# Normalise-and-transpose in quarters, early weight loads and spread weight-statistics reductions in an attention-plus-FFN layer on eight cores

## The chip, the cores and the metric

One Trainium2 chip, eight cores, one program on all of them, each with its own data: core c works on batch c // 2 and owns the 2048 tokens of one parity of it. Nothing is exchanged between cores. The metric is the device time of the slowest core in microseconds (us).

## What is computed

The reference, cut to what matters (x is 4 x 4096 x 2048, 16 heads of 128, FFN width 5120):

```python
xn = layernorm(x)
q, k, v = xn @ Wq + bq, xn @ Wk + bk, xn @ Wv + bv      # per head, rope on q and k
attn = softmax(q k^T / sqrt(128)) * tril                 # mask after the softmax
a = (attn v) @ Wo + bo
h = square(relu(xn @ tern(w_fc)^T))
f = h @ tern(w_proj)^T
out = x + a + f
# tern(w): am = max(mean|w|, 1e-5); +am where w > 0.7 am, -am where w < -0.7 am, else 0
```

Because the mask comes after the softmax, all 4096 keys enter the denominator of each query, and only the causal ones enter the product with v. Because tern needs mean|w| over a whole matrix, both FFN matrices are read once in full for their sum of magnitudes (the statistics) before they are used.

## The kernel before

The program is written as five lists of closures, one per engine (SyncE, called SP in the profile, GpSimd = POOL, VectorE = DVE, ScalarE = ACT, TensorE = PE), and each engine runs its list in the order in which the Python code appended to it. Semaphores link the lists. So where a statement stands in the Python code sets what it is queued behind. It has stages, with a barrier after the V projection and after the heads, and later ones that the change leaves alone.

**Layernorm (L210 to L298).** 32 blocks of 128 tokens. SP loads x_t (two buffers; load tb waits for the ACT pass of block tb-2, L235), DVE sums (L240), ACT squares with an accumulated sum (L245), small operations give mean and reciprocal deviation, ACT writes xn_t in bf16 (L288), and POOL stores it to a DRAM scratch, xn_scr (L295). xn_t has two buffers, and the ACT pass of block tb waits for the store of block tb-2.

**Transposes (L316 to L327).** When all 32 stores have landed, SP issues 16 transposing DMAs, each of a 4096 x 128 column strip of xn_scr into xnT, which stays in SBUF with channels on partitions. Before them, POOL fetches the bias row bvr and PE and DVE spread it over the partitions (L300 to L315).

**V projection (L329 to L373).** Eight column groups (dch) of 256; POOL loads the weights wv_sl of a group (L339, two buffers, f32 in DRAM and bf16 in SBUF), and for each of 32 token blocks PE runs 16 matmuls (L352), DVE adds the bias into v_ev (L365, two buffers) and POOL stores it to v_scr (L371). The load of group dch stands in POOL's list behind all stores of group dch-1. Then SP loads the rope tables and POOL the q and k weights of head 0 (L385, L391), and a barrier waits for all of it.

**Heads (plan_head, 16 times).** POOL loads the q and k weights (L478, L485). Then come the statistics: 20 pieces of 256 KB per head, loaded by SP into stb (two buffers; load i waits for reduction i-2, emit_stat_load), and reduced by DVE for w_fc (L445, heads 0 to 7) or by ACT for w_proj (L456, heads 8 to 15). All 20 loads and 20 reductions stand at the front of a head's lists; SP's load of v_head (L500) stands behind the loads. After them come the projections. PE makes q in four strips of 512 tokens (L522), in two PSUM banks, so that strip j waits for the ACT eviction (L535) of strip j-2. A pair of strips goes through qe_b, a half swap by two POOL DMAs into qsw_b (L544, L545) and three DVE operations (L553, L554, L562: rope) before the next pair may be evicted into qe_b. The same is done four more times for k (L582, L595, L606, L607, L613, L614, L623). One such pass is called a rope piece here.

Then eight chunks of 256 queries. For each, eight groups of four key blocks: PE makes the scores (L664) in one of three PSUM regions and ACT exponentiates them (L687). Between the groups of chunk c PE does the rest of chunk c-1: the sums of the exponentials (L706), after which DVE masks (L724) and inverts (L759, 1.75 us), then the product with v (L743); DVE scales it (L770) and POOL stores it (L776). The exponentials of groups 0 to 3 of chunk c overwrite what the first half of L743 of chunk c-1 reads, and those of 4 to 7 what its second half reads.

**Later stages.** FFN in (L966), FFN out (L1067), output projection (L1158).

Of the kernel before, what the change touches and what calls it, by code (L numbers as in the profile page):

```python
# [89 lines left out]
def build_nc():  # L90
# [21 lines left out]
    def em(name, fn):  # L112
        streams[name].append(fn)
# [8 lines left out]
    with ExitStack() as S0:  # L122
# [39 lines left out]
        sxnt = dsem("sxnt")  # L162
# [5 lines left out]
        sstat = [dsem("sstat0"), dsem("sstat1")]  # L168
# [42 lines left out]
        with ExitStack() as S1:  # L211
# [13 lines left out]

            LNH = float(H)
            xn_act, xn_store = [], []
            for tb in range(NTB):
# [69 lines left out]
                xn_store.append(sxnc.inc())  # L298

            def f(g):  # L300
                g.dma_start(out=bvr_s[:], in_=d["bvr"]).then_inc(sbv.sem, 16)
            em("gpsimd", f)
            bvl = sbv.inc()
            def f(t, bvl=bvl, const_v=const_v):
                t.wait_ge(sbv.sem, bvl)
                t.wait_ge(sem_v, const_v)
                for j in range(4):
                    ins = t.matmul(psum[:, 2048+j*512:2048+(j+1)*512], ones_rb[0:1, :],
                                   bvr_s[0:1, j*512:(j+1)*512], start=True, stop=True)
                ins.then_inc(sem_t, 1)  # L310
            em("tensor", f); bvt = st.inc()
            def f(v, bvt=bvt):
                v.wait_ge(sem_t, bvt)
                v.tensor_copy(bvb[:], psum[:, 2048:4096]).then_inc(sem_v, 1)
            em("vector", f); bvb_ready = sv.inc()  # L315

            xn_all = (sxn[0].n, sxn[1].n)
            for cb in range(NCB):
                def f(sy, cb=cb, xn_all=xn_all):
                    if cb == 0:  # L320
                        sy.wait_ge(sxn[0].sem, xn_all[0])
                        sy.wait_ge(sxn[1].sem, xn_all[1])
                    sy.dma_start(out=xnT[:, cb*T:(cb+1)*T],  # L323
                                 in_=d["xn_scr"][:, cb*128:(cb+1)*128],
                                 transpose=True).then_inc(sxnt.sem, 16)
                em("sync", f)
                sxnt.inc()  # L327
            xnT_ready = sxnt.n

            wv_load, vproj_mm, vproj_ev, v_store = [], [], [], []  # L330
            for dch in range(8):
                buf = wv_sl[dch % 2]
                sl = d["wv"][:, dch*256:(dch+1)*256].rearrange("(cb p) n -> p cb n", p=128)
                war = (dch - 2 + 1) * NTB - 1 if dch >= 2 else None
                swvc = swv[dch % 2]
                def f(g, sl=sl, buf=buf, war=war, swvc=swvc):
                    if war is not None:
                        g.wait_ge(sem_t, vproj_mm[war])
                    g.dma_start(out=buf[:].rearrange("p (cb n) -> p cb n", n=256),  # L339
                                in_=sl).then_inc(swvc.sem, 16)  # L340
                em("gpsimd", f)
                wv_load.append((swvc.sem, swvc.inc()))
                for tb in range(NTB):
                    bank = (tb % 2) * 512
                    idx = dch * NTB + tb
                    def f(t, dch=dch, tb=tb, bank=bank, idx=idx):
                        t.wait_ge(*wv_load[dch])
                        t.wait_ge(sxnt.sem, xnT_ready)
# [34 lines left out]
            sl = d["wq"][:, 0:128].rearrange("(cb p) n -> p cb n", p=128)  # L383
            def f(g, sl=sl):
                g.dma_start(out=wqk_q[:].rearrange("p (cb n) -> p cb n", n=128),  # L385
                            in_=sl).then_inc(swq.sem, 16)
            em("gpsimd", f)
            wq0_ld = swq.inc()
            sl = d["wk"][:, 0:128].rearrange("(cb p) n -> p cb n", p=128)
            def f(g, sl=sl):  # L390
# [848 lines left out]
```

## Time and profile before

| what | us |
| --- | --- |
| median of the 2 runs shown | 5806.05 (5696.27 and 5915.83) |
| the profiled execution | 5513.23 |
| its span on the slowest core (core 3) | 5511.7 |
| spans of the eight cores | 5440.3 to 5511.7 |

The profile is of core 3. PE is busy for 71% of the span, ACT 28%, DVE 22%, POOL 12%. "Busy" of PE counts overlapped matmuls in a modelled way; what each stage waits for has to be read from its own rows. The engines' idle time is put down to a releaser, the event that came last.

### The profile page before, as it was taken

How to read it: one execution, taken by the hardware profiler on the slowest of the kernel's cores; microseconds unless marked ns; L12 is line 12 of the kernel's file. 1: busy time of each engine (PE TensorE's matmuls, PEld its weight loads, DVE VectorE, ACT ScalarE, POOL GpSimd, SP SyncE). 2: the span in 40 equal slices, each digit the busy share in tenths (PEclk: the TensorE clock that was granted, in tenths of full speed). 3: DMA queues.
4: the chain of work that ended last, by engine and by line, in shares of the span. 5: the costliest groups of instructions: out<-in, count | busy, mean ns of one | idle time of the engine just before them, and what ended most of it. 6: DMA issues, size and time to landing. Idle time of an engine off the chain costs nothing.

```text
span 5511.7 us, 66436 instructions; the slowest of 8 cores (5440.3 to 5511.7 us)
## 1 busy us (share of the span) xinstructions
PE 3927.8 (71%) x23892; PEld 2334.3 (42%) x23892; DVE 1235.9 (22%) x1858; ACT 1570.2 (28%) x2017; POOL 688.2 (12%) x1218
## 2 busy tenths in 40 slices
PE   0058888666676676667666766676788886999788
PEld 0047676434443453345334533453433333444333
DVE  3201112222222222212111211121344440000011
ACT  6400000323432343344434434444333330000000
POOL 0012222000000000000000000000244331000000
PEclk9987789889998898899988988998999998999899
DMA  6751122132123202320232033203355556675664
GB/s 205 201 125 39 41 46 63 43 67 63 26 53 67 61 16 63 67 60 19 62 67 60 14 67 68 58 15 64 122 198 199 186 195 220 227 247 195 187 172 145
DMA packets 364633, 564.40 MB, mean 102 GB/s; under 512 B 226336, under 2 KB 259104, under 8 KB 341024
## 3 DMA queue, kind: packets, MB, share of 16 engines
q1 hardware_dynamic: 228128, 383.90, 23.1%
q0 software_dynamic: 136192, 176.25, 13.0%
q8 instruction: 206, 3.38, 0.3%
q14 instruction: 107, 0.88, 0.1%
HBM read 434.21 MB, written 117.44 MB: 100 GB/s over the span
## 4 chain that ended last, share of the span: by engine, by line
PE 52%; DMA 20%; ACT 9%; DVE 7%; issue 7%; POOL 3%; SPq 2%; ACTq 0%; DVEq 0%; another core or an unknown queue 0%; POOLq 0%
PE psum L1067 9%; PE psum L352 9%; PE psum L706 8%; PE psum L664 7%; PE psum L966 6%; ACT expT L687 5%; DMA stb<-wprT 5%; DMA stb<-wfcT 5%; PE psum L582 4%; PE psum L743 4%; PE psum L1158 4%; DMA qsw_b<-qe_b 2%; DMA x_t<-xp 2%; DMA hT_tc<-hT_scr 2%; SPq L323 2%
## 5 line engine op out<-in xcount | busy, mean ns | idle before, releaser
L687 ACT ACTIVATE expT<-psum 128x1024 bf16<-128x1024 f32 x1024 | 970.1, 1030 | 674.2 <-PE psum L743 620.6
L664 PE MATMUL psum<-qrotT,krotT 128*128 128x256 bf16 x4096 | 611.7, 282 | 377.3 <-ACT expT L687 282.6
L352 PE MATMUL psum<-wv_sl,xnT 128*128 128x256 bf16 x4096 | 516.3, 296 | 169.7 <-DMA xnT<-xn_scr 89.5
L966 PE MATMUL psum<-xnT,qfc 128*128 128x512 bf16 x2560 | 576.4, 388 | 84.7 <-DVE qfc L953 82.3
L664 PEld LDWEIGHTS psum<-qrotT,krotT 128*128 128x128 bf16 x4096 | 365.1, 100 | 564.5 <-issue 515.3
L1067 PE MATMUL psum<-qpr,hT_tc 128*128 128x512 bf16 x2560 | 559.7, 382 | 60.7 <-DMA hT_tc<-hT_scr 60.7
L582 PE MATMUL psum<-xnT,wqk_k 128*128 128x512 bf16 x2048 | 464.4, 387 | 162.4 <-ACT qe_b L535 150.5
L352 PEld LDWEIGHTS psum<-wv_sl,xnT 128*128 128x128 bf16 x4096 | 432.1, 106 | 254.5 <-issue 174.2
L706 PE MATMUL psum<-expT,ones_cb 128*128 128x256 bf16 x4096 | 500.8, 277 | 0.0
L522 PE MATMUL psum<-xnT,wqk_q 128*128 128x512 bf16 x1024 | 276.8, 439 | 294.1 <-DMA wqk_q<-wq 163.8
L706 PEld LDWEIGHTS psum<-expT,ones_cb 128*128 128x128 bf16 x4096 | 405.9, 99 | 52.8
L966 PEld LDWEIGHTS psum<-xnT,qfc 128*128 128x128 bf16 x2560 | 252.8, 100 | 407.9 <-issue 123.7
L1067 PEld LDWEIGHTS psum<-qpr,hT_tc 128*128 128x128 bf16 x2560 | 251.7, 98 | 368.8 <-issue 71.4
L582 PEld LDWEIGHTS psum<-xnT,wqk_k 128*128 128x128 bf16 x2048 | 199.9, 99 | 426.3 <-issue 205.5
L535 ACT ACTIVATE qe_b<-psum,bqc_s 128x512 bf16<-128x512 f32 x64 | 42.0, 684 | 1160.8 <-PE psum L522 915.5
L743 PE MATMUL psum<-expT,v_head 128*128 128x256 bf16 (+1 forms) x2304 | 278.8, 266 | 119.3 <-DVE expT L724 119.2
L522 PEld LDWEIGHTS psum<-xnT,wqk_q 128*128 128x128 bf16 x1024 | 110.8, 110 | 455.8 <-issue 370.7
L743 PEld LDWEIGHTS psum<-expT,v_head 128*128 128x128 bf16 x2304 | 207.6, 97 | 188.5 <-issue 157.5
L776 POOL DMA_DIRECT2D o_scr<-o_sb x128 | 69.9, 546 | 1696.7 <-DVE o_sb L770 1569.4
L1158 PE MATMUL psum<-wo_all,oT_t 128*128 128x512 bf16 x1024 | 232.1, 388 | 52.2 <-DMA wo_all<-wo 52.2
L365 DVE TENSOR_TENSOR v_ev<-psum,bvb 128x256 bf16<-128x256 f32 x256 | 108.7, 425 | 575.8 <-PE psum L352 517.1
L1002 POOL DMA_DIRECT2D hT_scr<-hT_t x320 | 183.1, 580 | 389.1 <-ACT hT_t L993 381.5
(82 smaller groups left out, 2296.5 us busy)
## 6 DMA issues: line engine op xcount, KB each, us to landing
hT_tc<-hT_scr SPq DMA_DIRECT2D x32, 2560.0 KB, 12.6
stb<-wfcT SPq DMA_DIRECT2D x160, 256.0 KB, 3.0
stb<-wprT SPq DMA_DIRECT2D x160, 256.0 KB, 3.0
wpr_b<-wprT SPq DMA_DIRECT2D x40, 1024.0 KB, 5.0
wfc_b<-wfc SPq DMA_DIRECT2D x40, 1024.0 KB, 7.2
x_t<-xp SPq DMA_DIRECT2D x32, 1024.0 KB, 8.2
qsw_b<-qe_b POOLq DMA_DIRECT2D x192, 128.0 KB, 2.4
qpr_scr<-qprs POOLq DMA_DIRECT2D x160, 128.0 KB, 2.2
```

Of the source, the lines that this page charges most:

```text
L323: sy.dma_start(out=xnT[:, cb*T:(cb+1)*T], in_=d["xn_scr"][:, cb*128:(cb+1)*128], transpose=True).then_inc(sxnt.sem, 16)
L352: ins = t.matmul(psum[:, bank:bank+256], xnT[:, cb*T + tb*128: cb*T + (tb+1)*128], wv_sl[dch % 2][:, cb*256:(cb+1)*256], start=(cb == 0), ...
L522: ins = t.matmul(psum[:, bank:bank+512], wqk_q[:, cb*128:(cb+1)*128], xnT[:, cb*T + j*512: cb*T + (j+1)*512], start=(cb == 0), stop=(cb == ...
L582: ins = t.matmul(psum[:, bank:bank+512], wqk_k[:, cb*128:(cb+1)*128], xnT[:, cb*T + tcol: cb*T + tcol + 512], start=(cb == 0), stop=(cb == ...
L664: ins = t.matmul(psum[:, reg+pos*256: reg+pos*256+256], krotT[:, kb*128:(kb+1)*128], qrotT[:, c*W:(c+1)*W], start=(pos % 2 == 0), stop=(po ...
L687: s.activation(expT[:, g0*W:(g0+4)*W], psum[:, reg:reg+1024], AF.Exp, scale=SCALE).then_inc(sem_s, 1)
L706: ins = t.matmul(psum[:, DF0:DF0+W], ones_cb[:], expT[:, kb*W:(kb+1)*W], start=(kb == 0), stop=(kb == 31))
L743: ins = t.matmul(psum[:, OT0+cs:OT0+256], v_head[:, kb*128:(kb+1)*128], expT[:, kb*W+cs:(kb+1)*W], start=(half == 0 and i == 0), stop=(hal ...
L966: ins = t.matmul(psum[:, reg + tc*512: reg + (tc+1)*512], qfc[fb % 2][:, cb*128:(cb+1)*128], xnT[:, cb*T + tc*512: cb*T + (tc+1)*512], sta ...
L1002: g.dma_start(out=d["hT_scr"][tcx][:, fb], in_=hT_t[fb % 2][:, tcx*256:(tcx+1)*256]).then_inc(shc.sem, 16)
L1067: ins = t.matmul(psum[:, reg:reg+512], lhs, qpr[q % 2][:, fb*512:(fb+1)*512], start=(fb == 0), stop=(fb == NFB-1))
L1158: t.matmul(psum[:, reg + cc*512: reg + (cc+1)*512], lhs, wo_all[:, ob*H + cc*512: ob*H + (cc+1)*512], start=(ob == 0), stop=False)
```

## The change

Line numbers of the changed kernel stand in the diff's own rows only; the prose keeps those of the kernel before. What it does:

- bvr, its matmuls and its copy, the first two loads of wv_sl and the q and k weights of head 0 go to the front of the lists, ahead of the layernorm.
- The transposes are cut into four quarters of 1024 tokens. After each eighth block of the layernorm loop, SP waits for the stores of all blocks so far and issues 16 transposes of 1024 x 128. Each quarter has a semaphore of its own, and a V-projection block waits for its own quarter alone.
- stb has three buffers. The 20 loads still stand at the front of a head on SP, while the reductions are taken from a list (RQ) between the groups of the chunk loop by reds_until: after group g of chunk c, (8c + g) * 20 // 64 of them are done.
- v_head is loaded by POOL, behind the q and k weights and ahead of the swaps.

```diff
+            emit_wv_load(0)
+            emit_wv_load(1)
+            sl = d["wq"][:, 0:128].rearrange("(cb p) n -> p cb n", p=128)
...
             for tb in range(NTB):
...
+                if (tb + 1) % 8 == 0:
+                    qt = tb // 8
+                    snap = (sxn[0].n, sxn[1].n)
+                    sxq = sxnt[qt]
+                    def f(sy, qt=qt, snap=snap, sxq=sxq):
+                        sy.wait_ge(sxn[0].sem, snap[0])
+                        sy.wait_ge(sxn[1].sem, snap[1])
+                        for cb in range(NCB):
+                            sy.dma_start(out=xnT[:, cb*T + qt*1024: cb*T + (qt+1)*1024],
+                                         in_=d["xn_scr"][qt*1024:(qt+1)*1024,
+                                                         cb*128:(cb+1)*128],
+                                         transpose=True).then_inc(sxq.sem, 16)
+                    em("sync", f)
...
             for dch in range(8):
+                if dch >= 2:
+                    emit_wv_load(dch)
                 for tb in range(NTB):
+                    qrd = xnq_ready[tb // 8]
-                        t.wait_ge(sxnt.sem, xnT_ready)
+                        t.wait_ge(*qrd)
...
-            stb = [E2(nc.sbuf_tensor(f"stb{i}", [128, 512], F32)) for i in range(2)]
+            stb = [E2(nc.sbuf_tensor(f"stb{i}", [128, 512], F32)) for i in range(3)]
...
                 for k in range(20*h, 20*h+20):
                     emit_stat_load(k)
-                    emit_stat_red(k)
+                RQ = list(range(20*h, 20*h+20))
+                def reds_until(done_groups, RQ=RQ):
+                    tgt = (done_groups * 20) // 64
+                    while (20 - len(RQ)) < tgt:
+                        emit_stat_red(RQ.pop(0))
...
-                em("sync", f)
+                    g.dma_start(out=v_head[:].rearrange("p (kb n) -> p kb n", n=128),
+                                in_=src).then_inc(svh.sem, 16)
+                em("gpsimd", f)
...
                     emit_group(c, 2)
+                    reds_until(c*8 + 3)
                     emit_group(c, 3)
...
                     emit_group(c, 4)
+                    reds_until(c*8 + 5)
                     emit_group(c, 5)
...
                     emit_group(c, 6)
+                    reds_until(c*8 + 7)
                     emit_group(c, 7)
+                    reds_until(c*8 + 8)
                 emit_p2(NCH-1)
+                while RQ:
+                    emit_stat_red(RQ.pop(0))
```

SP's list at the layernorm; L235 and L281 are the loads of x_t, L323 and L353 the transposes. Before:

```order
L235 DMA x_t<-xp 128x2048 x32
L323 DMA_TRANSPOSE xnT<-xn_scr 128x4096 x16
L378 DMA cos_s<-cos 128x4096
L379 DMA sin_s<-sin2s 128x4096
L435 DMA stb<-wfcT 128x512 x20
```

Now:

```order
L281 DMA x_t<-xp 128x2048 x8
L353 DMA_TRANSPOSE xnT<-xn_scr 128x1024 x16
L281 DMA x_t<-xp 128x2048 x8
L353 DMA_TRANSPOSE xnT<-xn_scr 128x1024 x16
L281 DMA x_t<-xp 128x2048 x8
L353 DMA_TRANSPOSE xnT<-xn_scr 128x1024 x16
L281 DMA x_t<-xp 128x2048 x8
L353 DMA_TRANSPOSE xnT<-xn_scr 128x1024 x16
```

The ninth load of x_t now stands behind the first 16 transposes, and so at each of three places.

ACT's list in a head of the second half of the heads, from the evictions of the head before it on; L456 and L469 are the reductions. Before:

```order
L595 ACTIVATE qe_b<-psum,bkc_s 128x512 x8
L687 ACTIVATE expT<-psum 128x1024 x64
L456 ACTIVATE dmp,prr<-stb 128x512 x20
L535 ACTIVATE qe_b<-psum,bqc_s 128x512 x4
L595 ACTIVATE qe_b<-psum,bkc_s 128x512 x8
```

Now, its first two chunks and a little more:

```order
L553 ACTIVATE qe_b<-psum,bqc_s 128x512 x4
L613 ACTIVATE qe_b<-psum,bkc_s 128x512 x8
L705 ACTIVATE expT<-psum 128x1024 x5
L469 ACTIVATE dmp,prr<-stb 128x512
L705 ACTIVATE expT<-psum 128x1024 x2
L469 ACTIVATE dmp,prr<-stb 128x512
L705 ACTIVATE expT<-psum 128x1024 x4
L469 ACTIVATE dmp,prr<-stb 128x512
L705 ACTIVATE expT<-psum 128x1024 x2
L469 ACTIVATE dmp,prr<-stb 128x512
L705 ACTIVATE expT<-psum 128x1024 x3
L469 ACTIVATE dmp,prr<-stb 128x512
```

The 20 reductions left the front and stand singly among the exponentials; DVE's are spread in the same manner in the first eight heads.

POOL's list between the V projection and the first swaps. Before:

```order
L371 DMA v_scr<-v_ev 128x256 x32
L385 DMA wqk_q<-wq 128x16x128
L391 DMA wqk_k<-wk 128x16x128
L544 DMA qsw_b<-qe_b 64x1024
```

Now:

```order
L396 DMA v_scr<-v_ev 128x256 x32
L517 DMA v_head<-v_scr 128x32x128
L562 DMA qsw_b<-qe_b 64x1024
L563 DMA qsw_b<-qe_b 64x1024
```

The two weight loads have gone ahead of the layernorm, and the load of v_head stands directly ahead of the first swap.

## Rows read from the trace of the kernel before

**Rows 1.** Windows by stage: length, busy us of PE, PEld, DVE, ACT, POOL, PEclk, DMA, GB/s.

```profile
0.00:243.00 243.00, 0.00 (x0) 0.00 (x0) 88.91 (x135) 150.88 (x161) 19.04 (x38) 1.00 0.67 208
243.00:336.00 93.00, 1.86 (x4) 0.42 (x4) 2.29 (x1) 0.00 (x0) 0.00 (x0) 1.00 1.01 192
336.00:945.00 609.00, 516.30 (x4096) 432.11 (x4096) 108.67 (x256) 0.00 (x0) 148.53 (x265) 0.83 0.20 46
945.00:2427.00 1482.00, 1003.76 (x6738) 640.13 (x6739) 380.67 (x684) 549.51 (x612) 101.00 (x173) 0.90 0.23 51
2427.00:3920.00 1493.00, 1023.28 (x6848) 651.96 (x6846) 279.43 (x542) 660.91 (x924) 104.40 (x177) 0.91 0.24 52
```

**Rows 2.** Waits of PE over the span: total us, times, longest.

```profile
PE psum L664 <- ACT expT L687: 282.6, 427, 2.0
...
PE psum L522 <- DMA wqk_q<-wq: 163.8, 15, 11.9
...
PE psum L522 <- ACT qe_b L535: 117.4, 8, 16.7
PE psum L352 <- DMA xnT<-xn_scr: 89.5, 1, 89.5
...
PE psum L352 <- DMA wv_sl<-wv: 78.3, 7, 11.4
...
PE psum L522 <- DMA wqk_k<-wk: 12.8, 1, 12.8
```

**Rows 3.** Timeline, end of the layernorm: start, length, engine, operation.

```profile
233.65 1.91 ACT L245 ACTIVATE dump<-x_t 128x2048 bf16<-128x2048 f32 x1 [1.35 <-DMA x_t<-xp]
...
237.74 2.10 ACT L288 ACTIVATE xn_t<-x_t,negmr,rstd 128x2048 bf16<-128x2048 f32 x1 [0.41 <-DVE negmr L277]
...
243.49 91.03 SPq L323 DMA_TRANSPOSE xnT<-xn_scr  x16
```

**Rows 4.** DMA issues: queue, count, KB each, median us to landing.

```profile
x_t<-xp SPq DMA_DIRECT2D x32, 1024.0 KB, 8.2
qsw_b<-qe_b POOLq DMA_DIRECT2D x192, 128.0 KB, 2.4
...
v_scr<-v_ev POOLq DMA_DIRECT2D x256, 64.0 KB, 1.8
v_head<-v_scr SPq DMA_DIRECT2D x16, 1024.0 KB, 7.3
...
wv_sl<-wv POOLq DMA_DIRECT2D x8, 1024.0 KB, 9.1
wqk_q<-wq POOLq DMA_DIRECT2D x16, 512.0 KB, 8.7
```

**Rows 5.** Groups over the span: count, busy us, mean ns, idle before and its releasers.

```profile
L456 ACT ACTIVATE dmp<-stb 128x512 bf16<-128x512 f32 x160 | 101.0, 631 | 220.5 <-DMA stb<-wprT 218.8
...
L535 ACT ACTIVATE qe_b<-psum,bqc_s 128x512 bf16<-128x512 f32 x64 | 42.0, 684 | 1160.8 <-PE psum L522 915.5 <-DVE qrotT L562 245.3
...
L456 ACT ACTIVATION_READ_ACCUMULATOR dmp<-stb 128x1 f32 x160 | 30.1, 188 | 0.0
```

**Rows 6.** Waits in heads 0 to 7 (945 to 2427 us).

```profile
ACT qe_b L535 <- DVE qrotT L562: 190.8, 8, 30.8
```

**Rows 7.** Timeline of DVE, front of head 3.

```profile
1542.54 0.69 DVE L445 TENSOR_REDUCE fcr<-stb 128x1 f32<-128x512 f32 x1 [0.17 <-DMA stb<-wfcT]
1543.14 0.68 DVE L553 TENSOR_TENSOR rt<-qe_b,cos_s 128x1024 bf16<-128x1024 bf16 x1
```

**Rows 8.** Timeline of PE, front of head 10.

```profile
3186.50 9.93 PE L522 MATMUL psum<-xnT,wqk_q 128*128 128x512 bf16 x32 [11.86 <-DMA wqk_q<-wq]
3208.85 9.00 PE L522 MATMUL psum<-xnT,wqk_q 128*128 128x512 bf16 x32 [12.42 <-ACT qe_b L535]
```

**Rows 9.** Chain of waits in the chunk loop of head 10.

```profile
3308.38 1.95 ACT expT L687 x2
```

More of the change, by code:

```diff
@@ L161, in build_nc @@
         sbv = dsem("sbv")
-        sxnt = dsem("sxnt")
+        sxnt = [dsem(f"sxnt{i}") for i in range(4)]
         swv = [dsem("swv0"), dsem("swv1")]
@@ L224, in build_nc, with f @@
             v_ev = [E1(nc.sbuf_tensor(f"v_ev{i}", [128, 256], BF16)) for i in range(2)]
+            def f(g):
+                g.dma_start(out=bvr_s[:], in_=d["bvr"]).then_inc(sbv.sem, 16)
+            em("gpsimd", f)
+            bvl = sbv.inc()
+            def f(t, bvl=bvl, const_v=const_v):
+                t.wait_ge(sbv.sem, bvl)
+                t.wait_ge(sem_v, const_v)
+                for j in range(4):
+                    ins = t.matmul(psum[:, 2048+j*512:2048+(j+1)*512], ones_rb[0:1, :],
+                                   bvr_s[0:1, j*512:(j+1)*512], start=True, stop=True)
+                ins.then_inc(sem_t, 1)
@@ new lines, in build_nc, with f, emit_wv_load @@
+            em("tensor", f); bvt = st.inc()
+            def f(v, bvt=bvt):
+                v.wait_ge(sem_t, bvt)
+                v.tensor_copy(bvb[:], psum[:, 2048:4096]).then_inc(sem_v, 1)
+            em("vector", f); bvb_ready = sv.inc()
+            wv_load, vproj_mm, vproj_ev, v_store = [], [], [], []
+            def emit_wv_load(dch):
+                buf = wv_sl[dch % 2]
+                sl = d["wv"][:, dch*256:(dch+1)*256].rearrange("(cb p) n -> p cb n", p=128)
+                war = vproj_mm[(dch - 1) * NTB - 1] if dch >= 2 else None
+                swvc = swv[dch % 2]
+                def f(g, sl=sl, buf=buf, war=war, swvc=swvc):
+                    if war is not None:
+                        g.wait_ge(sem_t, war)
+                    g.dma_start(out=buf[:].rearrange("p (cb n) -> p cb n", n=256),
+                                in_=sl).then_inc(swvc.sem, 16)
+                em("gpsimd", f)
+                wv_load.append((swvc.sem, swvc.inc()))
@@ new lines, in build_nc, with f @@
+            emit_wv_load(0)
+            emit_wv_load(1)
+            sl = d["wq"][:, 0:128].rearrange("(cb p) n -> p cb n", p=128)
+            def f(g, sl=sl):
+                g.dma_start(out=wqk_q[:].rearrange("p (cb n) -> p cb n", n=128),
+                            in_=sl).then_inc(swq.sem, 16)
+            em("gpsimd", f)
+            wq0_ld = swq.inc()
+            sl = d["wk"][:, 0:128].rearrange("(cb p) n -> p cb n", p=128)
+            def f(g, sl=sl):
+                g.dma_start(out=wqk_k[:].rearrange("p (cb n) -> p cb n", n=128),
+                            in_=sl).then_inc(swk.sem, 16)
@@ L298, in build_nc @@
                 xn_store.append(sxnc.inc())
[L300 to L325, printed above, removed]
-                em("sync", f)
-                sxnt.inc()
@@ L328, in build_nc @@
-            xnT_ready = sxnt.n
-            wv_load, vproj_mm, vproj_ev, v_store = [], [], [], []
-            for dch in range(8):
[L332 to L342, printed above, removed]
+                if (tb + 1) % 8 == 0:
[11 more added lines that the diff above has]
+                    em("sync", f)
+                    for _ in range(NCB):
+                        sxq.inc()
+                    xnq_ready.append((sxq.sem, sxq.n))
@@ L515, in f @@
                         if h == 0 and j == 0:
-                            t.wait_ge(sxnt.sem, xnT_ready)
+                            for _sw, _sv in xnT_ready:
+                                t.wait_ge(_sw, _sv)
                         if j == 0 and qkb_war is not None:
```

45 lines of the change are left out of this document (17 added, 28 removed).

## The prediction

> **What bounds the kernel now.** I read the windows by stage first [rows 1]. In the first 336 us PE does nothing: 243 us are layernorm with the DMA engines busy for 0.67 of the time, then come 93 us in which nothing runs but the transposes, at a DMA share of 1.01 and 192 GB/s. The V projection takes 609 us with 516 us of PE work. The heads take 1482 and 1493 us, some 186 us each, with only 1004 and 1023 us of PE work: the heads hold about 950 us of idle PE. The stages behind them are not touched. Next I read who PE waits for [rows 2]. Of the heads' waits, 282.6 us go to the exponentials, in short pieces (427 times), 163.8 us to the load of the q weights (about 11 us a head), and 117.4 us in eight long pieces to the eviction of q. In the V projection there are seven waits for wv_sl, 11 us each. Last I read a head's front on the engine that is late there. In heads 0 to 7 the first rope operation starts right behind the last reduction of DVE [rows 7], though its q strips were ready long before. In heads 8 to 15 PE makes two q strips and then stands for 12.4 us, because the eviction is queued behind ACT's reductions [rows 8].
>
> So two things the change touches are on the path: the transposes, and a head's front. The question is what it puts on the path in their place.
>
> **The layernorm and its transposes.** Now PE starts V at 336 us, after 89.5 us of waiting for xnT [rows 1, 2]. In the changed order SP's loads stand behind the transposes three times. One stop is priced so. After the last ACT pass ended (237.74 + 2.10 = 239.84 us) SP went on at 243.49: 3.65 us until the store had landed [rows 3]. A quarter of the transposes is a quarter of SP's 91.03 us [rows 3], 22.8 us, if their price goes by bytes; it is the nearest row, and the full DMA share of that window speaks for bytes. Then x_t needs 8.2 us to land [rows 4]. Together 34.6 us, against the 1.35 us that ACT stood idle before the last block [rows 3]: 33 us each, 99 us for three. From below, a price by bytes can hardly fall, as the share is 1 already; from above, it is 5.7 us an instruction whatever its size (91.03 / 16), which makes a quarter 91 us. I take 22.8.
>
> At the start, POOL's queue now holds two wv_sl loads and the q and k loads ahead of the first store of xn. By [rows 4] they are 9.1 us each and 8.7 us for a pair of half that size that shares the queue: some 27 us alone, and more beside the x_t loads. Block 2 can't be written before store 0 has landed. Bounds are 0 (all of it in the 33% of DMA time that is free) and 27 us; I take 15.
>
> Layernorm on DVE thus ends 114 us later, at about 351 us. Does PE start earlier on the first quarters? Only by two blocks: V's evictions stand on DVE behind the whole layernorm loop, and there are two banks. Two blocks are 2 x 516.3 / 256 = 4 us [rows 1]. So V starts in effect at 347 us, 10 us later than now; the last quarter's 22.8 us are hidden behind the 24 blocks (48 us) on the other three. While they run, stores of v_ev slow down; I add 5 us. Then two gains: the second wv_sl load is there already (one of seven waits, -11 us [rows 2]), and the 12.8 us wait for head 0's weights shrinks to the landing of the last store, eviction and issue included about 4.5 us (v_scr lands in 1.8 us [rows 4]), -8 us. **This part: +15 - 11 - 8 = -4 us**, between -30 and +220.
>
> *A page's figure beside this.* The trace moved the transposes at 192 GB/s [rows 1]. The Trainium skill, page "DMA: Bandwidth & Descriptors", section "Latency and other measured facts", gives an effective 261 GB/s for a transposing DMA with a non-contiguous middle dimension. By that figure, an estimate, a quarter would take 17 us and the sum fall by 17 us more; the trace doesn't bear it out here, and the sum goes by the trace.
>
> **The front of heads 0 to 7.** The eviction of the third q strip waits for the first rope piece: 190.8 us in these eight heads [rows 6], against 245.3 over all sixteen [rows 5], so 54.5 us in the other eight, where DVE was free. With reductions gone from DVE's front the first eight should wait like the others: **-136 us** (190.8 - 54.5), 17 us a head. The rope pieces behind it cycle through qe_b, the swap and DVE, and keep their rhythm. Spread out, a reduction takes 0.69 us [rows 7] in a DVE that is busy for 381 of 1482 us [rows 1]; each stands where DVE's next mask or scaling still waits for PE. I cost them at 0; if that cover fails, 160 of them are 110 us.
>
> **The front of heads 8 to 15.** PE waited 117.4 us for the q eviction [rows 2], all of it behind ACT's reductions. Next late is the first rope piece, which moves with the eviction. **-117 us.** But ACT now has the reductions inside the loop, 631 + 188 = 0.82 us each [rows 5]. In a chunk the chain runs through the exponentials of groups 4 to 6 (1.95 us for two of them in one link [rows 9]), while those of groups 0 to 3 and 7 lie beside PE work, with ACT idle behind them until the product with v frees their buffer. Of the four places, the one behind group 4 is on that chain; the rule (8c + g) * 20 // 64 fills it in each of the eight chunks, and in chunk 0 one more stands where ACT alone is the pace. Nine a head: 9 x 0.82 x 8 = **+59 us**. Bounds are 0 and all twenty, 131 us; nine is the count that the chain gives.
>
> **v_head behind POOL.** It takes 7.3 us to land [rows 4], and is first needed behind all projections of the head. But the first swap stands behind it. The q weights land, PE makes two strips (9.93 us [rows 8]), ACT evicts: the swap comes about 11 us after the q weights. In that time the k weights (11.5 us, issued right behind: about 4 us behind the q weights [rows 4]) and v_head (7.3) have to pass, 11 to 12 us. I take 2 us of delay a head, **+32 us**, between 0 and 7.3 us (+117). In return the weights no longer share the DMA engines with the statistics: I let the q load (8.7 us [rows 4]) fall to the 7.3 us that v_head's megabyte takes, 1.4 x 15 = **-21 us**, between 0 and twice that.
>
> **Sum.** -4 - 136 - 117 + 59 + 32 - 21 = -187 us on the profiled execution's 5513.2 us: 5326 us, 0.966 of it. The median of the two runs shown lies 5% above the profiled execution, and I take the ratio over to it: 5806 x 0.966 = **5609 us**.
>
> **Rivals.**
>
> *A: the transposes are priced by the instruction (slower).* At 5.7 us each a stop is 68 us longer, three are +205 us, and the last quarter (91 us) outlasts the 48 us of V work by some 43 us: the sum becomes -187 + 205 + 43 = +61 us, 5574 us, or 5870 us at the median. For it speaks that the 16 instructions took about equal times; against it, the DMA share of 1.01, which an issue limit would not give. It decides from about 4.5 us an instruction on.
>
> *B: the loop and the swap eat it.* All twenty ACT reductions count (+72 us more) and v_head stands fully before the first swap (+85 more): -30 us, 5483 us, or 5774 us at the median; half of this already leaves less than 2%. For it speaks that PE waits 427 times for exponentials [rows 2]. Against it, ACT is busy for only 661 of 1493 us in these heads [rows 1]. The Trainium skill bears on the swap, page "DMA: Bandwidth & Descriptors", section "Queues, rings and completion order": a DMA engine takes turns between queues at packet boundaries, and within one queue it consumes in ring order. By that rule v_head on SP's queue shares with the swap, and on POOL's it stands before it. No row of this trace shows the two on one queue.
>
> *C: the fronts have another floor.* If the rope cycle and not the reductions sets a front, the -136 and -117 shrink to nothing much: some 5500 us, 5790 at the median. The difference between the first and the last eight heads in the same wait [rows 5, 6] speaks against it.
>
> **Chances.** Forecast 0.72, A 0.07, B 0.17, C 0.04. A difference of 2% is about what a measurement of this kernel can tell from none. My forecast's own range in the profiled frame is -270 (reductions hidden, swap free) to -60 us (half of B, or a stop 30 us longer each), at the median 5522 to 5743 us. The two runs shown differ from their median by 1.9%, so I let the low end down to 5440; A is left out. Faster by over 2%: 0.73, the forecast and a little of B; within 2%: 0.20; slower: 0.07.
>
> **What would show it.** Right: SP holds 16 transposes for about 23 us four times, with x_t loads stopped meanwhile; V begins near 350 us; the wait of the q eviction for qrotT is about 7 us in every head; the 117.4 us wait of PE is gone; heads 0 to 7 take about 169 us and heads 8 to 15 about 179 us. Wrong: a stop of over 60 us (A); a wait of DVE's first rope operation for qsw_b that is 5 us longer than in heads 8 to 15 now, or a chunk of heads 8 to 15 that is over 1.5 us longer than one of heads 0 to 7 (B); fronts as long as before (C).

## The result and the profile after

| | before | changed |
| --- | --- | --- |
| median of all runs | 5511.9 us (10 runs) | 5341.05 us (13 runs) |
| lowest | 5467.78 us | 5234.52 us |
| ratio | | 0.9566, 95% interval 0.9552 to 0.958 |

In some executions one die of the chip runs TensorE at a lower granted clock and both medians hold such runs, so the ratio and all comparisons below use runs, or the dies of a run, without it: there the kernel before takes about 5475 us and the changed kernel about 5237.

The change makes the kernel 4.3% faster, some 238 us. Forecast were 3.4% (187 us) and a median of 5609 us with a range from 5440: the direction and most of the mechanism held, the time did not.

To compare stage by stage I take cores whose span is near these times: core 4 of before (5470.3 us) and core 3 of the changed kernel (5231.1 us). Windows by stage of before's core 4 (length, busy us of PE, PEld, DVE, ACT and POOL, granted clock, DMA share, GB/s): to the start of V, V projection and barrier, heads 0 to 7, heads 8 to 15, the rest.

```profile
0.00:332.00 332.00, 1.86 (x4) 0.41 (x4) 91.08 (x136) 150.19 (x161) 19.05 (x38) 1.00 0.78 206
332.00:899.00 567.00, 469.08 (x4097) 408.09 (x4098) 108.30 (x256) 0.00 (x0) 148.56 (x265) 0.91 0.22 49
899.00:2385.00 1486.00, 1006.35 (x6784) 642.31 (x6782) 383.13 (x688) 550.52 (x617) 101.09 (x174) 0.91 0.23 52
2385.00:3887.00 1502.00, 1021.61 (x6800) 649.62 (x6800) 283.83 (x542) 658.09 (x920) 106.83 (x181) 0.90 0.24 53
3887.00:5470.00 1583.00, 1382.29 (x6208) 609.95 (x6208) 368.81 (x237) 208.12 (x320) 312.48 (x561) 0.95 0.60 197
```

The same stages of the changed kernel, core 3:

```profile
0.00:350.00 350.00, 8.20 (x36) 4.84 (x36) 91.51 (x138) 148.81 (x161) 22.02 (x40) 0.67 0.76 188
350.00:908.00 558.00, 464.54 (x4064) 404.10 (x4064) 107.88 (x255) 1.75 (x1) 145.44 (x263) 0.92 0.25 55
908.00:2232.00 1324.00, 994.31 (x6784) 640.18 (x6784) 362.79 (x688) 548.51 (x608) 115.22 (x183) 0.95 0.25 58
2232.00:3645.00 1413.00, 1027.66 (x6800) 656.32 (x6800) 284.40 (x542) 644.59 (x928) 119.64 (x188) 0.92 0.25 57
3645.00:5231.00 1586.00, 1380.10 (x6208) 609.09 (x6208) 368.37 (x236) 209.19 (x320) 312.55 (x561) 0.95 0.58 196
```

The first two stages together got 9 us longer (899 to 908), the first eight heads 162 us shorter, the last eight 89 us shorter, the rest 3 us longer. PE's work in each is what it was: all of the difference is idle time in the heads. V took 567 us on this core of before; on core 3, which the rows ahead of the prediction show, it took 609 [rows 1], with PE busy for 516 us at a granted clock of 0.83, against 469 us at 0.91 here. Part of what I priced from was a slower clock on that core.

PE's waits, core 3 of the changed kernel (total us, times, longest), which answer to [rows 2]:

```profile
PE psum L682 <- ACT expT L705: 297.8, 409, 2.0
PE psum L377 <- DVE v_ev L390: 247.2, 14, 230.6
PE psum L540 <- DMA wqk_q<-wq: 141.1, 15, 10.7
...
PE psum L377 <- DMA xnT<-xn_scr: 106.4, 1, 106.4
...
PE psum L377 <- DMA wv_sl<-wv: 69.9, 6, 13.1
```

The wait for the q eviction is gone from the list, one of seven waits for wv_sl too. The wait for the q weights went from 163.8 to 141.1 us. The 230.6 us are those in which PE, two V blocks done, waits for DVE to leave the layernorm. So the early start on the quarters was worth two blocks and no more, as the order of DVE's list had said.

SyncE's own timeline of the changed kernel (start, length):

```profile
2.91 65.55 SPq L281 DMA_DIRECT2D x_t<-xp  x8
86.33 22.23 SPq L353 DMA_TRANSPOSE xnT<-xn_scr  x16
108.67 47.59 SPq L281 DMA_DIRECT2D x_t<-xp  x8
174.09 23.63 SPq L353 DMA_TRANSPOSE xnT<-xn_scr  x16
197.83 47.01 SPq L281 DMA_DIRECT2D x_t<-xp  x8
261.89 25.96 SPq L353 DMA_TRANSPOSE xnT<-xn_scr  x16
287.95 50.69 SPq L281 DMA_DIRECT2D x_t<-xp  x8
355.52 29.86 SPq L353 DMA_TRANSPOSE xnT<-xn_scr  x16
```

A quarter takes 22.2 to 29.9 us against the 22.8 of the forecast: between these two sizes the price goes by bytes, and rival A falls. The last quarter is the longest here. V's stores run beside it, but they ran beside the last quarter of e5 and e8 below too, which took 25.6 and 25.7 us; so that they are the reason isn't shown.

For the heads I split each into a front, from the issue of the q weights to the end of the last k eviction, and a loop, the rest. Means in us, read from the timelines of POOL and ACT:

| | front, heads 1 to 7 | front, 8 to 15 | loop, 1 to 7 | loop, 8 to 14 |
| --- | --- | --- | --- | --- |
| before (core 4) | 75.0 | 73.1 | 111.4 | 112.5 |
| changed (core 3) | 54.5 | 54.0 | 112.0 | 120.2 |

The same fronts cut into their steps, on the same cores. Each column is the time from the step before it; the last one ends with the last k eviction.

| heads | issue of the q weights to first q matmul | to the eviction of the second q strip | to both halves of the first swap landed | to the last operation of the first rope piece | to the end |
| --- | --- | --- | --- | --- | --- |
| 1 to 7, before | 9.5 | 9.4 | 5.5 | 17.3 | 33.3 |
| 1 to 7, changed | 8.0 | 9.2 | 4.2 | 1.6 | 31.5 |
| 8 to 15, before | 9.3 | 24.5 | 6.1 | 1.6 | 31.6 |
| 8 to 15, changed | 7.5 | 9.2 | 4.2 | 1.6 | 31.5 |

Most of the gain is where it was forecast: the rope no longer waits for DVE (17.3 to 1.6 us), the eviction no longer for ACT (24.5 to 9.2 us). The first swap (two DMAs on POOL, a half each) got faster too: from its issue, 1.3 us behind the eviction, to the landing of both halves it took 4.9 us in heads 8 to 15 and takes 2.9 (4.2 and 2.9 in heads 1 to 7). In head 12 of before, core 4, v_head was issued 5.2 us ahead of it and landed 2.1 us behind its issue:

```profile
3156.18 0.39 SPq L500 DMA_DIRECT2D v_head<-v_scr  x1
...
3161.41 0.55 POOL L544 DMA_DIRECT2D qsw_b<-qe_b  x1 [33.51 <-ACT qe_b L535]
...
3166.19 0.69 DVE L553 TENSOR_TENSOR rt<-qe_b,cos_s 128x1024 bf16<-128x1024 bf16 x1 [41.72 <-DMA qsw_b<-qe_b]
```

In the changed kernel, core 3, v_head landed 2.5 us before the first swap of this head was issued, and the rope follows the swap by 3.0 us and not by 4.8:

```profile
2948.03 0.55 POOL L562 DMA_DIRECT2D qsw_b<-qe_b  x1 [13.77 <-ACT qe_b L553]
...
2950.99 0.69 DVE L571 TENSOR_TENSOR rt<-qe_b,cos_s 128x1024 bf16<-128x1024 bf16 x1 [21.86 <-DMA qsw_b<-qe_b]
```

### The profile page after: what moved, and what is told of

Its sections match the earlier page's. It is cut to its first block, busy times and chain, and to the rows that moved or that the text cites. A ratio compares the mean times of both kernels' runs of the same rounds, so it can differ in the third digit from the quotient of the medians.

```text
span 5296.6 us, 66567 instructions; the slowest of 8 cores (5211.5 to 5296.6 us)
## 1 busy us (share of the span) xinstructions
PE 3937.6 (74%) x23892; PEld 2326.8 (44%) x23892; DVE 1215.3 (23%) x1858; ACT 1549.9 (29%) x2017; POOL 715.1 (14%) x1234
## 4 chain that ended last, share of the span: by engine, by line
PE 57%; DMA 14%; ACT 9%; issue 8%; DVE 7%; POOL 3%; SPq 1%; another core or an unknown queue 0%; ACTq 0%; DVEq 0%; POOLq 0%
PE psum L1091 10%; PE psum L724 9%; PE psum L377 7%; PE psum L682 7%; PE psum L990 6%; ACT expT L705 5%; PE psum L1182 5%; PE psum L761 5%; PE psum L600 4%; DMA qsw_b<-qe_b 3%; PE psum L540 3%; DMA wqk_q<-wq 2%; DMA x_t<-xp 2%; DMA hT_tc<-hT_scr 2%; POOL hT_scr L1026 2%
## 5 line engine op out<-in xcount | busy, mean ns | idle before, releaser
L705 ACT ACTIVATE expT<-psum 128x1024 bf16<-128x1024 f32 x1024 | 982.3, 1028 | 638.7 <-PE psum L761 583.4
L377 PE MATMUL psum<-wv_sl,xnT 128*128 128x256 bf16 x4096 | 471.0, 279 | 418.6 <-DVE v_ev L390 242.9
L1091 PE MATMUL psum<-qpr,hT_tc 128*128 128x512 bf16 x2560 | 579.0, 391 | 64.8 <-DMA hT_tc<-hT_scr 64.8
L377 PEld LDWEIGHTS psum<-wv_sl,xnT 128*128 128x128 bf16 x4096 | 407.9, 100 | 482.4 <-issue 426.1
L724 PE MATMUL psum<-expT,ones_cb 128*128 128x256 bf16 x4096 | 517.9, 282 | 0.0
L600 PE MATMUL psum<-xnT,wqk_k 128*128 128x512 bf16 x2048 | 449.9, 379 | 20.8 <-ACT qe_b L613 11.4
L540 PE MATMUL psum<-xnT,wqk_q 128*128 128x512 bf16 x1024 | 255.9, 417 | 159.7 <-DMA wqk_q<-wq 155.4
L1182 PE MATMUL psum<-wo_all,oT_t 128*128 128x512 bf16 x1024 | 277.8, 443 | 53.5 <-DMA wo_all<-wo 53.5
L794 POOL DMA_DIRECT2D o_scr<-o_sb x128 | 69.7, 545 | 1757.2 <-DVE o_sb L788 1599.3
L777 DVE RECIPROCAL rb_sb<-psum 128x256 f32<-128x256 f32 x128 | 224.1, 1751 | 0.6 <-DVE expT L742 0.6
```

The lines of the kernel that those rows point to most:

```text
L377: ins = t.matmul(psum[:, bank:bank+256], xnT[:, cb*T + tb*128: cb*T + (tb+1)*128], wv_sl[dch % 2][:, cb*256:(cb+1)*256], start=(cb == 0), ...
L540: ins = t.matmul(psum[:, bank:bank+512], wqk_q[:, cb*128:(cb+1)*128], xnT[:, cb*T + j*512: cb*T + (j+1)*512], start=(cb == 0), stop=(cb == ...
L600: ins = t.matmul(psum[:, bank:bank+512], wqk_k[:, cb*128:(cb+1)*128], xnT[:, cb*T + tcol: cb*T + tcol + 512], start=(cb == 0), stop=(cb == ...
L705: s.activation(expT[:, g0*W:(g0+4)*W], psum[:, reg:reg+1024], AF.Exp, scale=SCALE).then_inc(sem_s, 1)
L724: ins = t.matmul(psum[:, DF0:DF0+W], ones_cb[:], expT[:, kb*W:(kb+1)*W], start=(kb == 0), stop=(kb == 31))
L777: v.reciprocal(rb_sb[:], psum[:, DF0:DF0+W]).then_inc(sem_v, 1)
```

## The experiments

Each kernel is compared with the changed one (5237 us) and with the kernel before on the same chip. Ratios are to before. The chips differ: the kernel before took 5472 to 5477 us on that of e1 to e4, but 5486 to 5499 us on that of e5, e6, e8 and e10, and 5491 to 5501 us on that of e7 and e11. So a time in us that is set against 5237 us is off by 10 to 25 us in these last six; the ratios are not. "Heads" is the time from the first q matmul to the first of the FFN: 2989 us before and 2736 us in the changed kernel, on the two cores above.

### Whole transposes again (e1)

```diff
-                if (tb + 1) % 8 == 0:
-                    ... 16 transposes of 1024 x 128
+            for cb in range(NCB):      # behind the layernorm loop
+                    ... one transpose of 4096 x 128
```

> The changed kernel, but the transposes are again 16 whole strips behind the last layernorm block; early weight loads, three stb buffers, spread reductions and v_head on POOL stay. Theory: the quarters are worth nothing, since each of three stops costs as much as the hidden quarter gives back. The layernorm then ends 14.5 us later than before (257 us), the transposes take 93 us more, and V starts near 350 us, as in the changed kernel; the time is 5237 us within 10. Rival: the quarters are a part of the gain (PE on the first quarters early), and without them the time is 40 us or more longer, 5277 us. Second rival: the stops cost more than they give back, and the time falls by over 15 us.

5213.8 and 5215.6 us, ratio 0.9525 (0.9484 to 0.9566). SyncE's timeline on core 3:

```profile
2.91 233.97 SPq L281 DMA_DIRECT2D x_t<-xp  x32
255.53 82.59 SPq L351 DMA_TRANSPOSE xnT<-xn_scr  x16
```

The transposes took 83 us and not 91, with the weight loads no longer beside them, and V started at 340.4 us. The first q matmul came at 884 us, against 909 in the changed kernel; the heads were the same (2732 us). So the quarters don't contribute: they cost 22 us, the second rival, a little over its bound. It is still a small effect, and the intervals of the two ratios overlap slightly; the two lowest runs of each lie 21 us apart, and the stage's own times show where it is. The three stops are the smaller part: DVE wrote its first block of V at 344.0 us here and at 349.5 us in the changed kernel. But from there to the first q matmul V took 540 us here and 559 us there. In its first 70 us, in which the last quarter is moved, PE was busy for 69.1 and 55.8 us (first row here, second the changed kernel):

```profile
340.00:410.00 70.00, 69.14 (x616) 60.81 (x617) 16.12 (x38) 0.00 (x0) 19.94 (x37) 1.00 0.20 65
350.00:420.00 70.00, 55.82 (x467) 46.96 (x468) 12.16 (x29) 1.75 (x1) 16.68 (x31) 0.95 0.62 126
```

### All reductions on DVE (e2)

```diff
-                if i < 160:
-                    ... reduce_sum on vector
-                else:
-                    ... Abs with accum_out on scalar
+                ... reduce_sum on vector, into fcr or prr
```

> The changed kernel, but DVE does the reductions of heads 8 to 15 as well, at the same places of the code. Theory: on ACT the reduction behind group 4 (and one more in chunk 0) lies on the chain, which made the chunk loops of heads 8 to 14 7.8 us longer a head (112.5 to 120.2 us) while those of heads 1 to 7 grew by 0.5 us with DVE's; so the loops of heads 8 to 15 come down to about 113 us, and the time falls by 8 x 7.3 = 58 us to 5179 us. Rival: the longer loops come from the statistics' traffic or from PE and not from where the reduction stands on ACT; then the loops stay at 120 us and the time within 10 us of 5237.

5174.9 us at the lowest, ratio 0.9484 (0.9409 to 0.9558); heads 2668 and 2671 us on two cores, 65 us less. The loops of heads 8 to 14 take 111.7 us, as long as those of heads 1 to 7 (112.1). The theory held.

### No reduction behind group 4 on ACT (e6)

```diff
-                    reds_until(c*8 + 5)
+                    if h < 8:
+                        reds_until(c*8 + 5)
```

> The changed kernel, but in heads 8 to 15 no reduction stands behind group 4; those move behind group 6 (two in a row there at times) and the rest stays on ACT. Theory: it is the place that costs and not ACT's work: behind group 6 the exponential that follows is not waited for at once, so the loops of heads 8 to 14 fall from 120.2 to about 114 us and the time by 40 to 55 us, to some 5190 us. Rival: ACT's work as such counts, 20 x 0.82 us a head half hidden wherever it stands; then the loops stay above 118 us and the time within 15 us of 5237.

5186.7 and 5187.8 us, ratio 0.9444 (0.9417 to 0.9472); heads 2673 us; loops of heads 8 to 14 111.9 us, less than was expected. ACT does the same work and the whole penalty is gone. One more count falls with it: the prediction held a ninth reduction, the one in chunk 0 that is not behind group 4, to cost as much. It stands behind group 6, e6 has two there, and they cost nothing. Here is ACT's timeline of the changed kernel, one chunk of head 11 (start, length, line, idle before):

```profile
2884.77 1.02 ACT L705 ACTIVATE expT<-psum 128x1024 bf16<-128x1024 f32 x1 [1.26 <-PE psum L761]
2885.69 0.62 ACT L469 ACTIVATE dmp<-stb 128x512 bf16<-128x512 f32 x1
...
2886.30 2.84 ACT L705 ACTIVATE expT<-psum 128x1024 bf16<-128x1024 f32 x3
2889.02 0.65 ACT L469 ACTIVATE dmp<-stb 128x512 bf16<-128x512 f32 x1
...
2893.17 3.78 ACT L705 ACTIVATE expT<-psum 128x1024 bf16<-128x1024 f32 x4 [3.41 <-PE psum L761]
```

The reduction at 2885.69 stands between exponentials that PE is waiting for and pushes them back by 0.6 us or more; the one at 2889.02 is followed by 3.4 us in which ACT waits for PE anyway. In e6 two reductions lie around the last exponential of a burst:

```profile
2889.04 3.05 ACT L705 ACTIVATE expT<-psum 128x1024 bf16<-128x1024 f32 x3 [2.42 <-PE psum L761]
2891.98 0.62 ACT L469 ACTIVATE dmp<-stb 128x512 bf16<-128x512 f32 x1
...
2892.59 1.01 ACT L705 ACTIVATE expT<-psum 128x1024 bf16<-128x1024 f32 x1
2893.50 0.63 ACT L469 ACTIVATE dmp<-stb 128x512 bf16<-128x512 f32 x1
```

### v_head back on SyncE (e3)

```diff
+                ... v_head loaded by sync, ahead of the statistics loads
                 for k in range(20*h, 20*h+20):
                     emit_stat_load(k)
-                ... v_head loaded by gpsimd
```

> The changed kernel, but v_head is loaded by SP again, ahead of the head's 20 statistics loads. Theory: behind the q and k weights on POOL's queue v_head cost nothing (swaps landed in 2.3 us as before), and it kept out of the way of the q weights; on SP it shares the DMA engines with them, the q weights land 2 to 4 us later than the 7.2 us of the changed kernel, the front of a head grows by as much, and the time rises by 30 to 60 us. Rival, the step of the prediction: v_head ahead of the first swap costs 2 us a head, which comes back here: the time falls by some 32 us, to 5205 us.

The lowest run took 5295.2 us, 58 more than the changed kernel; it is a single time, without an interval. Heads 2790 us, 54 more; fronts 57.8 and 57.5 us, 3.4 more. PE's wait and the landing of the q weights on core 3:

```profile
PE psum L540 <- DMA wqk_q<-wq: 193.4, 15, 13.4
```

```profile
wqk_q<-wq POOLq DMA_DIRECT2D x16, 512.0 KB, 10.8
```

In the changed kernel it is 141.1 us, and the issues read:

```profile
qsw_b<-qe_b POOLq DMA_DIRECT2D x192, 128.0 KB, 2.3
v_head<-v_scr POOLq DMA_DIRECT2D x16, 1024.0 KB, 12.7
wqk_q<-wq POOLq DMA_DIRECT2D x16, 512.0 KB, 7.2
```

The swaps land in 2.3 us there at the median, as before, and both halves of a head's first swap in 2.9 us in either kernel (4.9 us in heads 8 to 15 of before). v_head takes 12.7 us and not 7.3 [rows 4], which nobody waits for. The step of the prediction that charged 2 us a head for it is refuted. This run isn't the placement of before, though: there v_head stood behind the statistics loads and was issued 31 us after the q weights, here 1.6 us ahead of them. So the 54 us are what the changed kernel would lose by this other place, and not a gain over before.

### Reductions in front again, with three buffers and with two (e4, e11)

```diff
                     emit_stat_load(k)
+                    emit_stat_red(k)
-                RQ = list(range(20*h, 20*h+20))
+                RQ = []
```

> The changed kernel, but all 20 reductions of a head stand at its front again, with the loads (three buffers stay, v_head stays on POOL, early loads and quarters stay). Theory: the whole gain of the heads comes from this one step: fronts go back from 54 us to about 72 (the three buffers let the loads run a little closer together than two did) and the loops of heads 8 to 15 from 120 to 112 us; the time rises by 18 x 16 - 8 x 8 = 224 us to 5460 us. Rival: three buffers and v_head's move are a good part of it; then the fronts only go back to some 62 us and the time stays under 5370 us.

5386.1 us at the lowest, ratio 0.9881 (0.9782 to 0.998). Heads 2885 to 2899 us on three cores, fronts 69.7 and 66.0 us, loops 112.5 and 111.3. The rise is some 150 us, not 224: spreading is a large part of the gain but not all of it. The second kernel takes the third buffer away as well.

```diff
-            stb = [... for i in range(3)]
+            stb = [... for i in range(2)]
-                    if i >= 3:
-                        war = stat_red_done[i - 3]
+                    if i >= 2:
+                        war = stat_red_done[i - 2]
```

> The kernel of e4 (all reductions at a head's front), with two stb buffers and not three. Theory: of the 95 us by which e4's heads were shorter than those of the kernel before (2890 against 2989 us), the third buffer gave some 60 to 80: with two, a load waits for the reduction two before it, and the fronts go back from 70 and 66 us to about 74 and 72. The time rises by 60 to 80 us to 5450 to 5470 us. Rival: it was v_head, which no longer stands among the last loads on SP; then the fronts stay within 1.5 us of e4's and the time within 25 us of e4's 5386.

5551.6 us at the lowest, ratio 1.0122 (1.0069 to 1.0174): 1.2% slower than before. Heads 3039 to 3060 us. Cores differ more here than elsewhere, so I take means over all eight:

| | front, heads 1 to 7 | front, 8 to 15 | heads in all |
| --- | --- | --- | --- |
| before | 74.7 | 72.6 | 2982 |
| e11, two buffers in front | 78.6 | 77.0 | 3048 |
| e4, three buffers in front | 69.6 | 66.4 | 2890 |
| changed, three buffers, spread | 54.5 | 54.1 | 2738 |

The third buffer gives 9.1 and 10.5 us a head where the reductions stand in front, more than was expected. And this kernel's fronts are 3.9 and 4.4 us longer than before's, though its heads differ from before's only in v_head. DVE's reductions in a front of this kernel, on its slowest core, 6:

```profile
1495.10 0.69 DVE L458 TENSOR_REDUCE fcr<-stb 128x1 f32<-128x512 f32 x1 [0.18 <-DMA stb<-wfcT]
1505.19 0.69 DVE L458 TENSOR_REDUCE fcr<-stb 128x1 f32<-128x512 f32 x1 [9.41 <-DMA stb<-wfcT]
```

One statistics load held DVE for 9.4 us while the q, k and v_head loads were in flight; the longest such wait in the same head was 6.6 us on core 3 of this kernel and 6.0 us on core 4 of before. This core is the extreme one (its fronts of heads 1 to 7 take 80.7 us), but DVE waits longer in all in the quieter core too: 30.6 us for the statistics loads of a front on core 3 against 28.0 us on core 4 of before. So v_head on POOL early in a head costs some 4 us where the reductions stand in front, and costs nothing where they are spread.

### The early weight loads, later (e5)

```diff
-            emit_wv_load(0)
-            emit_wv_load(1)
-            ... q and k weights of head 0
...
                 xn_store.append(sxnc.inc())
+                if tb == 9:
+                    emit_wv_load(0)
+                if tb == 17:
+                    emit_wv_load(1)
+                if tb == 25:
+                    ... q and k weights of head 0
```

> The changed kernel, but the early loads stand further back on POOL: wv_sl 0 behind the store of block 9, wv_sl 1 behind that of block 17, the q and k weights of head 0 behind that of block 25. Theory: at the very start they held the first store of xn back by 15 us (block 2 was stored at 47.7 us and not at 32.8), and later they find room; the first quarter's transposes start near 72 us and not at 86, V starts near 338 us and not at 350, and the time falls by 12 us to 5225 us. Rival: each costs as much wherever it stands (the layernorm waits for its loads anyway), and the time stays within 4 us of 5237.

The lowest run took 5251.7 us, 15 more than the changed kernel, again a single time. On this chip the kernel before took 5486 us at the lowest, 19 more than at the lowest in the comparison above, so the 15 us are no difference. The expected fall of 12 us isn't there: a miss. On core 7 the first quarter started earlier, as expected, and the last did not:

```profile
68.78 24.76 SPq L356 DMA_TRANSPOSE xnT<-xn_scr  x16
...
357.11 25.60 SPq L356 DMA_TRANSPOSE xnT<-xn_scr  x16
```

17.6 us were won at the start and lost again on the way. The rival's reading fits: the layernorm lives on its transfers, and these loads cost it as much wherever they stand.

### Two loads of x_t ahead of each quarter (e8)

```diff
                 ld = sxc.inc()
+                if tb % 8 == 1 and tb >= 9:
+                    emit_quarter_tr(tb // 8 - 1)
...
-                if (tb + 1) % 8 == 0:
-                    ... transposes of this quarter
```

> The changed kernel, but each of the first three quarters of transposes stands two x_t loads later on SP, behind the loads that the two buffers allow anyway. Theory: a stop then costs some 19 us and not 33, because blocks 8q+8 and 8q+9 are loaded before the transposes begin; three stops save 42 us, V starts near 308 us, and the time falls to 5195 us, which is also below the kernel with whole transposes (5214). Rival: the transposes take all of the DMA engines, the two loads wait in them all the same, and the time falls by less than 15 us.

5226.3 and 5233.2 us, and the lowest is 8 less than the changed kernel's lowest. The quarters began at 91.4, 172.5, 252.3 and 328.1 us: 79 us apart, against 90 us in the changed kernel. The last began 27 us earlier, so two thirds of the expected 42 us are there at this place, and the first q matmul came 23 us sooner (881 us against 904, means of cores 0 to 3). The 8 us at the end understate that, as this chip is slower: set against before's lowest run on the same chip the lowest run is 0.9526 here (5226.3 to 5486.5), 0.9528 with whole transposes (5213.8 to 5472.2) and 0.9573 for the changed kernel (5234.5 to 5467.8). Between theory and rival, and as good as whole transposes, not better.

### The q and k weights a head ahead (e10)

```diff
-                    ... loads of the q and k weights at the head's own front
...
                     reds_until(c*8 + 8)
+                    if c == 3 and h + 1 < NH:
+                        emit_w_loads(h + 1, mil)
```

> The changed kernel, but POOL loads the q and k weights of the next head behind the fourth store of o of this one, when their buffers have long been read. Theory: PE's wait for the q weights (141 us in 15 heads) was one for an issue that stood behind the last store of the head; it goes, the fronts shrink by 9 us, and the time falls by 130 us to about 5105 us. Rival: with the q weights there, the first swap comes earlier and meets v_head on POOL's queue, so that 3 us or more of it come back in each head: the swaps' longest landing rises over 6 us and the fall is under 90 us.

5080.0 us at the lowest, ratio 0.9263 (0.9236 to 0.929). Heads 2576 and 2582 us, 157 us less. The wait for the q weights has left PE's list, and the swaps' longest landing is 4.1 us, so the rival falls. Stage windows on core 0, to the first q matmul, the heads, the rest:

```profile
0.00:916.00 916.00, 472.05 (x4100) 408.02 (x4100) 199.06 (x392) 150.30 (x161) 167.53 (x304) 0.83 0.43 105
916.00:3498.00 2582.00, 1998.76 (x13584) 1295.07 (x13584) 646.50 (x1230) 1191.57 (x1536) 235.06 (x370) 0.96 0.28 61
3498.00:5092.00 1594.00, 1387.58 (x6208) 611.42 (x6208) 368.68 (x237) 207.77 (x320) 312.63 (x561) 0.94 0.58 195
```

PE is now busy for 1999 of the heads' 2582 us. The buffers of the weights had been free for over 100 us, the length of the chunk loop; only the place in POOL's list held the load back.

### Three of them together (e7)

> Three steps together on the changed kernel: transposes whole (e1), all reductions on DVE (e2), q and k weights loaded a head ahead (e10). Theory: they lie in different places (front of the program, chunk loops, head fronts) and add up: 5237 - 23 - 63 - 150 = some 5000 us, 0.913 of the kernel before. Rival: with shorter fronts and loops DVE's reductions meet their loads or masks, and a part of the 63 us comes back: above 5030 us.

4998.9 us at the lowest, ratio 0.91 (0.9074 to 0.9127): 239 us less than the changed kernel, and the fastest version here. Heads 2507 us. The parts add up. What PE still waits for, core 1:

```profile
PE psum L374 <- DMA xnT<-xn_scr: 340.3, 1, 340.3
PE psum L669 <- ACT expT L692: 230.8, 370, 1.9
```

## Why the prediction was wrong

**The median frame.** This is the step that put the time out of the range. The sum was made against the profiled 5513 us and the ratio then laid on the 5806 us median of the two runs shown. Those two were not typical: over ten runs before's median is 5512 us, and over thirteen the changed kernel's is 5341, below the low end of 5440. The sum alone, 5326 us, was 1.7% above the 5237 us of like runs. Two runs that both lie over 3% above a profiled execution of the same program should have been weighed against it, and the profiled value put inside the range.

Once ratio and base are of the same kind the sum is not far off: 5475 x 0.966 = 5289 us against 5237. That 5326 us lies near the measured median of 5341 us is luck. The rest is sizes: -187 us were forecast and 238 measured.

**v_head on POOL, +2 us a head: the term of the sum that was wrong in sign.** It cost the swaps nothing and rid the first one of a neighbour. In heads 8 to 15 the first swap takes 2.9 us and not 4.9; e11, where v_head is on POOL and the reductions stand in front, has 3.0 there, so it is v_head's going and not the reductions'. I had v_head pass the swap's issue by 2 us; it lands 2.5 us before it in head 12. The rule on ring order that I set beside rival B plays no part for the swap, which comes when v_head is through. By the Trainium skill, page "DMA: Bandwidth & Descriptors", section "Queues, rings and completion order", what is on another queue takes turns. The rows fit this: the q weights land in 7.2 us with v_head behind them on their own queue and in 10.8 us with v_head on SyncE's (e3). But in e3 v_head is also issued 1.6 us ahead of them, and no run tells turns from this head start.

**Fronts of heads 0 to 7, -17 us each: right.** The sum with the q load's -1.4 and v_head's +2 made -16.4; measured -20.5. By the table of steps, the way to the first rope piece got 17.2 us shorter (32.2 to 15.0 us behind the first q matmul) and the q weights came 1.5 us sooner. What is left is v_head's +2, which isn't there, and 1.8 us in the rope pieces behind the first, which I had keep their rhythm. No run shows the cause of these.

**Fronts of heads 8 to 15, -14.6 us each: right.** Forecast with the same two terms -14.0, measured -19.2. The eviction of the second q strip comes 15.3 us sooner, and PE's wait for it was 122.3 us in eight heads on this core of before, also 15.3 us each: the wait was the shift. The other 3.8 us are the first swap (2.0) and the q weights (1.8). With v_head's +2 the two gaps are some 33 us and 42 us, more than the 51 us by which the sum was short; the layernorm gives 14 of them back.

**Layernorm and transposes, -4 us: the mechanism held, the size did not.** Measured +10 us up to the first q matmul. Held with its number: the price of a quarter, the 15 us at the start (block 2 stored at 47.7 us and not at 32.8), V's start near 350 us, two early V blocks, one less wait for wv_sl. Too small was the 5 us for V beside the last quarter: PE lost 13 us in those 70 us (e1). e1 adds what I had not drawn from my own sum: if three stops cost about what the last quarter hides, the quarters have no purpose.

**Reductions in ACT's loop, +7.4 us a head: right in size.** Measured +7.8 (120.2 against 112.5). But eight reductions make it and not nine, those behind group 4, at about 1 us each and not 0.82; e2 and e6 show the place. DVE's, costed at 0, took 0.5 us a head. Heads 1 to 7 now take 166.5 us and heads 8 to 15 174.2; forecast were 169 and 179.

**What was left out.** The third buffer had no term, because spreading makes it idle in the front. By the path of e11 and e4 the steps of the first eight heads' fronts are +3.9 us (v_head on POOL), -9.1 (third buffer), -15.1 (spreading), together -20.3, and over all heads +66, -158 and -152 us. What the third buffer is worth once the reductions are spread no run shows, so the share of each hangs on the order of this path.

**Rivals.** A fell by the price of a quarter, B by the swaps (the loops of heads 8 to 15 are 1 us longer a chunk, under its mark of 1.5), C by the fronts. C's price was also added up wrongly: without the -136 and -117 the sum is +66 us, 5579 us or 5875 at the median, and not 5500 and 5790. No other number hangs on it.

## What to carry to other kernels

Work that stands at the front of a serial chain on an in-order engine should be spread into that engine's waits, and where it goes decides its price: the same ACT reduction cost 1 us behind group 4 and nothing behind group 6. Before cutting a transfer into pieces for overlap, ask which queue the pieces will stop and whether the consumer's other engine is free to go on; here three stops, and a V projection that runs slower beside the last quarter, paid for one hidden quarter. A load that nobody waits for still slows what is in flight beside it: v_head's old place cost the first swap 2 us a head. And a load that waits at a stage boundary is often held by its place in the list and not by its buffer: moving two issues was worth as much as two thirds of the whole change.

## What was not expected of the hardware

Where a load is issued acted as a priority: behind the q weights on their own queue the megabyte of v_head left them at 7.2 us and took 12.7 us itself; issued 1.6 us ahead of them on SyncE's queue it made them 10.8 us and took 7.0. With the reductions in front and two buffers (e11), the statistics loads of 256 KB, 2.8 us at the median, took up to 12.3 us on core 6 (9.0 on core 3; 8.6 on core 4 of before) when they met such a burst.
